# Triangle layer t1: the mask goes into the operand of the projection instead of the product behind it

## The reference, cut to what matters

```python
def _L1_conv_ref(z, mask, w_ap, b_ap, w_ag, b_ag, w_bp, b_bp, w_bg, b_bg, w_g, b_g, w_z, b_z, ...):
    m = mask[..., None]
    zn = _layer_norm(z, ln_in_w, ln_in_b)
    a = (zn @ w_ap + b_ap) * jax.nn.sigmoid(zn @ w_ag + b_ag) * m
    b = (zn @ w_bp + b_bp) * jax.nn.sigmoid(zn @ w_bg + b_bg) * m
    x = jnp.einsum('bikc,bjkc->bijc', a, b)
    x = _layer_norm(x, ln_out_w, ln_out_b) @ w_z + b_z
    g = jax.nn.sigmoid(zn @ w_g + b_g)
    return x * g
```

## Time and profile before

| | us |
|---|---|
| median of the runs (3) | 526.87 |
| lowest and highest of them | 526.49, 528.16 |
| the profiled execution, its own time | 530.72 |
| its span in the profile | 528.9 |
| its granted TensorE clock, mean | 0.89 |

### The profile page before, as it was taken

One profiled execution on the slowest core, in us unless ns is written; L12 is line 12 of the kernel. 1 busy time (PEld: TensorE's weight loads), 2 busy tenths in 40 slices (PEclk: granted clock), 3 DMA queues, 4 the chain that ended last, 5 costly groups with the idle time before them and its releaser, 6 DMA issues.

```text
span 528.9 us, 8984 instructions
## 1 busy us (share of the span) xinstructions
PE 426.9 (81%) x3226; PEld 326.1 (62%) x3226; DVE 360.4 (68%) x1170; ACT 235.4 (44%) x577; POOL 250.6 (47%) x315
## 2 busy tenths in 40 slices
PE   3698867987798877998499968698598857869995
PEld 2466754566345753896399945598455846836664
DVE  4977688647996488547534458301968498998885
ACT  1597554620775546677300038476379543300000
POOL 4899288003985186000000035000879168269994
PEclk9999998778798989999589979799579996569999
DMA  9400000000000000000000000000000000001223
GB/s 171 84 2 1 1 1 0 1 3 0 1 2 1 0 2 0 1 2 2 1 0 1 1 2 1 0 2 2 0 1 2 1 0 1 2 0 20 42 45 55
DMA packets 34671, 6.05 MB, mean 11 GB/s; under 512 B 33713, under 2 KB 34369, under 8 KB 34626
## 3 DMA queue, kind: packets, MB, share of 16 engines
q1 hardware_dynamic: 34626, 5.46, 5.9%
HBM read 3.36 MB, written 2.10 MB: 10 GB/s over the span
## 4 chain that ended last, share of the span: by engine, by line
PE 53%; DVE 32%; ACT 5%; POOL 4%; issue 3%; DMA 1%; SPq 1%; DVEq 0%; POOLq 0%
PE psum L1606 7%; DVE moments L339 6%; PE psum L605 5%; PE psum L1179 5%; PE psum L1178 5%; DVE ab L762 4%; PE psum L476 4%; PE psum L634 3%; PE psum L645 3%; PE psum L1779 3%; DVE ab L746 3%; POOL z L401 2%; PE psum L1799 2%; PE psum L1784 2%; PE psum L1201 1%
## 5 line engine op out<-in xcount | busy, mean ns | idle before, releaser
L325 POOL TENSOR_TENSOR z<-x_cols,moments 128x496 f32<-128x496 f32 x28 | 30.4, 1086 | 80.6 <-DVE moments L339 80.6
L605 PE MATMUL psum<-wp_L,z_t 64*128 64x320 f32 x384 | 65.3, 472 | 1.3 <-DVE ab L762 0.9
L476 PE MATMUL psum<-ident,z 128*128 128x128 f32 x224 | 45.0, 339 | 21.4 <-POOL z L401 15.2
L339 DVE BATCH_NORM_STATS2 moments<-x_cols 128x6 f32<-128x64 f32 x448 | 60.9, 207 | 2.0 <-ACT x_cols L885 1.8
L476 PEld LDWEIGHTS psum<-ident,z 128*128 128x128 f32 x224 | 32.2, 174 | 45.1 <-POOL z L401 27.4
L605 PEld LDWEIGHTS psum<-wp_L,z_t 64*128 64x128 f32 x384 | 34.9, 196 | 26.0 <-issue 23.1
L378 ACT ACTIVATE z_t<-psum 128x512 f32<-128x512 f32 x56 | 40.2, 719 | 21.3 <-PE psum L476 20.8
L1314 ACT ACTIVATE ab<-psum,mv 128x128 f32<-128x128 f32 x108 | 39.7, 368 | 16.2 <-PE psum L1179 5.9
L824 POOL TENSOR_TENSOR gate<-gate,stats 128x512 f32<-128x512 f32 x24 | 25.2, 1049 | 45.2 <-DVE stats L787 44.8
L1179 PE MATMUL psum<-ab,R_vt 128*128 128x128 f32 x216 | 45.7, 294 | 0.0
L645 PE MATMUL psum<-wo_L,z_t 64*128 64x128 f32 x384 | 30.4, 301 | 18.5 <-DVE x_cols L795 11.5
(11 more groups left out here) (271 smaller groups left out, 894.7 us busy)
## 6 DMA issues: line engine op xcount, KB each, us to landing
x_cols<-in_x_dram SPq DMA_DIRECT2D x16, 128.0 KB, 2.9
out_dram<-x_rows SPq DMA_DIRECT2D x32, 64.0 KB, 1.9
par<-in_par_dram SPq DMA_DIRECT2D x1, 644.5 KB
w<-in_w_dram SPq DMA_DIRECT2D x4, 64.0 KB, 2.3
w<-in_w_dram SPq DMA_DIRECT2D x1, 256.0 KB, 2.5
mask<-in_mask_dram SPq DMA_DIRECT2D x1, 64.0 KB, 3.1
row<-in_row_dram SPq DMA_DIRECT2D x1, 3.3 KB
w_bias<-in_w_dram SPq DMA_DIRECT2D x1, 8.0 KB, 1.8
```

The source lines that it names most:

```text
L339: m = dve.bn_stats(moments[:, q, k:k + 2, :].rearrange("p k m -> p (k m)"), X4[:, SQ * q + s, g:g + 2, :].rearrange("p g c -> p c g"))
L476: m = pe.transpose(bank(b % 2)[:, k * N:(k + 1) * N], block_of(Z)(4 * b + k), ident[:, :])
L605: m = pe.matmul(bank(slot_bank(s) + h, 2 * 5 * C), ZT[rows, s, :], wp[l][rows, :, :], start=True, stop=True)
```

## The change

The mask is applied before the projection. Since a masked linear part is (zn @ w + bias) * m, and the bias goes through the operand too (one of the channel columns of `z` is set to ones, L396, so that a masked operand masks the bias as well), the linear columns can be computed from a masked copy of ZT. For this the mask has to lie as ZT does, channels on partitions and positions along the row, the same on all 32 channels:

- TensorE transposes the mask once (in `tri_weights_pe` of t1), and VectorE copies the result to `mask_turned` (in `tri_weights2_dve` of t1).
- SyncE stores it to a DRAM buffer of 64 KB, and after f0 has read its pooled values, four transfers read it back, each spread over 32 partitions, 32 x 4096, into the tile `gate` (MASK_WIDE). Step s of the loop later overwrites just the columns whose masked block was made.
- `masked_turned(eng, b)` multiplies a block of ZT by MASK_WIDE into the tile `squares` (ZTM): blocks 0 to 2 on VectorE, each ahead of product s = b, blocks 3 to 7 on GpSimd, each ahead of a gate pair.
- `project(s)` of t1 waits for masked block s//4 and makes three calls instead of one for each row half: sigmoid columns (2x64) and gate columns (2x32) from ZT, linear columns (2x64) from ZTM.
- The product of t1 is the one operation of t0 and t3.

```diff
@@ -134,6 +134,8 @@
         par = sb("par", [GC, NPAR])
         row = sb("row", [1, NROW])
         mask = sb("mask", [N, N])
+        mask_turned = sb("mask_turned", [N, N])
+        mask_rows = nc.dram_tensor("mask_rows_dram", (N, N), F32, kind="Internal").ap()
         stats = sb("stats", [N, 4, N])
         moments = sb("moments", [N, Q, SQ * G, 3])
         ident = sb("ident", [N, N])
@@ -285,6 +287,9 @@
         for L, first, ahead_of in ((t0, 3, (1, 3, 5, 8, 11)), (t1, 3, (1, 3, 5, 8, 11)), (t3, 5, (2, 4, 7))):
             L.turned_first, L.turn_ahead = first, {s: first + k for k, s in enumerate(ahead_of)}
         f0.outputs_of, r1.outputs_of = t0, t1
+        mask_ps, mask_copied = t0.s["bt_ps"], t0.s["bt_dve"]
+        zm_dve, zm_pool = t0.s["bt_dve"], t0.s["bt_act"]
+        mask_rows_in, mask_wide_in = x_in[0], x_in[1]
         t3.banks_free = x_done(r2)
         f3.early_banks_free = [output_read(t3, S // 4 - 3)]
         f3.banks_free = [output_read(t3, S // 4 - 1)]
@@ -562,6 +567,9 @@
             dve.tensor_copy(wo[l][:, 1, :], cent[:, :]).then_inc(sm, 1)
             if L is t0:
                 dve.tensor_copy(gate_cent[:, :], bank(L.wbank)[:, 320:320 + E0]).then_inc(f0.s["w_gate"], 1)
+            if L is t1:
+                dve.wait_ge(mask_ps, C // 4 + 1)
+                dve.tensor_copy(mask_turned[:, :], bank(L.wbank)[:, 352:352 + N]).then_inc(mask_copied, 1)
 
         def tri_weights_pe(pe, L):
             l = L.name
@@ -573,6 +581,9 @@
             pe.matmul(bank(L.wbank)[:, 192:320], cent[:, :], wotmp[l][:, 0:GC], start=True, stop=True)
             if L is t0:
                 pe.matmul(bank(L.wbank)[:, 320:320 + E0], cent[:, :], pcol("gate"), start=True, stop=True)
+            if L is t1:
+                pe.wait_ge(par_in, PAR_LOADS)
+                pe.transpose(bank(L.wbank)[:, 352:352 + N], mask[:, :], ident[:, :]).then_inc(mask_ps, 1)
             fold_biases(pe, bank(L.wbank)[:, 0:5 * C], scaled[l][:, :], prow(f"{l}_b"), lnb_at[l][:, :], pcol(f"{l}_w", C))\
                 .then_inc(L.s["w_pe"], 1)
 
@@ -589,6 +600,22 @@
             o = slot_bank(s) * BANK
             return PSUM[:, o:o + 2 * BANK].rearrange("p (h f) -> p h f", h=2)[:, :, 0:2 * 5 * C]\
                 .rearrange("p h (g w) -> p h g w", g=2)
+
+        MASK_WIDE = GATE[:, :].rearrange("p (s n) -> p s n", s=S)
+        ZTM = SQR[:, :].rearrange("p (s n) -> p s n", s=S)
+        ZM_DVE = 3
+
+        def masked_turned(eng, b):
+
+            eng.wait_ge(mask_wide_in, 16 * G + 16 * G)
+            eng.wait_ge(t1.s["zt"], t1.at["zt"] + b + 1)
+            done = zm_dve if b < ZM_DVE else zm_pool
+            eng.tensor_tensor(ZTM[:, 4 * b:4 * b + 4, :], ZT[:, 4 * b:4 * b + 4, :], MASK_WIDE[:, 4 * b:4 * b + 4, :],
+                              ALU.mult).then_inc(done, 1)
+
+        def masked_at(b):
+
+            return (zm_dve, C // 8 + 2 + b) if b < ZM_DVE else (zm_pool, C // 8 + 1 + b - ZM_DVE)
 
         def tri_pe(pe, L):
             l = L.name
@@ -600,10 +627,16 @@
                     pe.wait_ge(L.s["lin"], L.at["lin"] + s - SLOTS + 2)
                 if s > last:
                     pe.wait_ge(L.s["lin"], L.at["lin"] + s - SLOTS + 1)
+                if L is t1:
+                    pe.wait_ge(*masked_at(s // 4))
                 for h in range(2):
                     rows = slice(h * HALF_ROWS, (h + 1) * HALF_ROWS)
-                    m = pe.matmul(bank(slot_bank(s) + h, 2 * 5 * C), ZT[rows, s, :], wp[l][rows, :, :],
-                                  start=True, stop=True)
+                    if L is t1:
+                        for w, z in ((slice(0, 2 * C), ZT), (slice(4 * C, 5 * C), ZT), (slice(2 * C, 4 * C), ZTM)):
+                            m = pe.matmul(slot(s)[:, h, :, w], z[rows, s, :], wp[l][rows, :, w], start=True, stop=True)
+                    else:
+                        m = pe.matmul(bank(slot_bank(s) + h, 2 * 5 * C), ZT[rows, s, :], wp[l][rows, :, :],
+                                      start=True, stop=True)
                 m.then_inc(L.s["proj"], 1)
 
 
@@ -739,28 +772,18 @@
             eng.tensor_tensor(x, x, x_of(L)[:, 4 * b:4 * b + 4], ALU.add)\
                 .then_inc(L.s["xb"], 1)
 
-        def masked_product(dve, s):
-
-            for g in range(G):
-                w = slice(g * 2 * C, (g + 1) * 2 * C)
-                m = dve.scalar_tensor_tensor(out=to_ab(s)[:, g, :], in0=slot(s)[:, g // 2, g % 2, 2 * C:4 * C],
-                                             scalar=mask[:, g * S + s:g * S + s + 1], in1=SIG[:, s % SLOTS, w],
-                                             op0=ALU.mult, op1=ALU.mult)
-            m.then_inc(t1.s["lin"], 1)
-
         def x_block(L, b):
 
             return by_block(L.src)[:, 4 * b:4 * b + 4]
 
         def tri_dve(dve, L, after):
             for s in range(S):
+                if L is t1 and s < ZM_DVE:
+                    masked_turned(dve, s)
                 dve.wait_ge(L.s["sig"], L.at["sig"] + s + 1)
                 sig = SIG[:, s % SLOTS, :].rearrange("p (h g w) -> p h g w", h=2, g=2)
-                if L is t1:
-                    masked_product(dve, s)
-                else:
-                    dve.tensor_tensor(to_ab(s).rearrange("p (h g) w -> p h g w", h=2), slot(s)[:, :, :, 2 * C:4 * C], sig,
-                                      ALU.mult).then_inc(L.s["lin"], 1)
+                dve.tensor_tensor(to_ab(s).rearrange("p (h g) w -> p h g w", h=2), slot(s)[:, :, :, 2 * C:4 * C], sig,
+                                  ALU.mult).then_inc(L.s["lin"], 1)
             if L is t0:
                 for b in range(1, C // 4, 2):
                     turn_copy(dve, L, b, BT[:, 4 * b:4 * b + 4, :], "bt_dve", "bt_ps")
@@ -813,6 +836,8 @@
         def tri_pool(pool, L, after):
             pool.wait_ge(L.s["w_dve"], L.at["w_dve"] + TRI_W)
             for b in range(S // 4):
+                if L is t1 and b + ZM_DVE < S // 4:
+                    masked_turned(pool, b + ZM_DVE)
                 gate_bias(pool, L, b)
                 add_x(pool, L, b)
             pool.wait_ge(L.s["xb"], L.at["xb"] + S // 4)
@@ -1974,6 +1999,13 @@
             sp.dma_start(w1_bias[:, :], w1_d[C:C + 1, :, :].rearrange("o e h -> (o e) h")).then_inc(par_in, 16)
             sp.dma_start(w2[:, :, :], w2_d).then_inc(par_in, 16)
             sp.dma_start(w2l[:, :], w2l_d).then_inc(par_in, 16)
+            sp.wait_ge(mask_copied, C // 8 + 1)
+            sp.dma_start(mask_rows, mask_turned[:, :]).then_inc(mask_rows_in, 16)
+            sp.wait_ge(mask_rows_in, 16 * G + 16)
+            sp.wait_ge(f0.s["pool_ps"], f0.at["pool_ps"] + 1)
+            for g in range(G):
+                sp.dma_start(MASK_WIDE[g * C:(g + 1) * C, :, :],
+                             mask_rows[g * S:(g + 1) * S, :].unsqueeze(0).to_broadcast([C, S, N])).then_inc(mask_wide_in, 16)
             out4 = out_d.rearrange("(g s) j c -> j g s c", g=G)
             for b in range(S // 4):
                 sp.wait_ge(f3.s["done"], f3.at["done"] + 2 * b + 2)
```

## The result

| | before | changed |
|---|---|---|
| median, us | 526.68 (4 runs) | 538.15 (4 runs) |
| lowest and highest | 525.19, 528.16 | 537.38, 538.78 |
| ratio, 95% interval | | 1.0204 [1.0161, 1.0247] |
| span of the profiled execution | 528.9 | 537.0 |

The change costs 11.5 us; the forecast was +2.0, with a range up to 537.0. The direction was right, the size was not.

What follows compares the result with a forecast made beforehand. VectorE was taken to bound the second half of the t1 stage, with TensorE replacing it. Copy near f0 +0.3, t1 stage +3.3, L634 -1.6: net +2.0, 528.9 us; range 525.6 to 537.0.

Steps and rivals of the forecast that it cites:

- half level at the start: TensorE at t1's start: after idling, the clock starts at half level, costing 2.5 us (1.95 to 3.05).
- 32p + turns + last pass: TensorE in t1's loop: 32 steps of p, five turns of 0.59 us, then a last pass of 0.26.
- masked block 0: VectorE ahead of t1's loop: the first 128x512 mask product takes 1.0 us, bounds 0.69 and 1.40.
- t1 later as a whole: Around gating layer f0, ahead of t1: VectorE's added mask copy delays later work by 0.3 us.
- p: TensorE's time per step in t1's loop: six weight loads of 0.113, 0.68 us, at most 0.82.
- L978: TensorE row of 4-column passes with 128-column weights, 0.113 us apart; taken as the price of one weight load.
- The first rival: t1's row halves do not run beside each other: 0.90 or 1.13 a step, 536.0 or 543.3 us; chance 0.13 + 0.12.
- The wait: At t1's start TensorE waits for VectorE's first masked block; first projection at 141.4, not 137.09.
- late and slow start: Start of t1's loop: first projection delayed by the masked block, then half clock; costs about 7 us together.
- L634: TensorE's outer product after t1's loop: near 7.4 us instead of 9.05, counted as -1.6.
- one copy near f0: VectorE copies the turned mask once behind t1's weight copies: 0.28 us, counted as +0.3.
- the transfers: Mask to DRAM and 2 MB spread back: there before 131, first read at 140.3, cost nothing.

Runs made afterwards that it cites:

- e5: The changed kernel plus five extra 512-column matmul calls filling TensorE's wait for the first masked block: 533.35 us, 1.0092 against the kernel before.
- e1: The kernel before with only t1's projection split into three calls per row half, no wait or mask transfer: 541.1 us, 1.0217.
- e2: The changed kernel with one 320-column call per row half again, all from the masked operand: 526.56 us, 0.9987 against the kernel before.
- e3: The changed kernel with two calls per row half, 192 columns from ZT and 128 from ZTM: 527.13 us, 1.0008 against the kernel before.
- e9: The changed kernel with each gate call widened from 64 to 128 columns, still twelve passes a step: 534.23 us, 1.0126 against the kernel before.
- e10: The changed kernel with a step's six calls alternating between the row halves: 530.79 us, 1.0060 against the kernel before.
- e8: The kernel before without t1's mask, one unmasked product a step: 519.41 us, 0.9867.
- e6: The changed kernel with two calls per row half and the first block as in the kernel before: 524.71 us, 0.9950 against the kernel before.
- e4: The changed kernel with steps 0 to 3 as in the kernel before, six calls from step 4: 524.87 us, 0.9948 against the kernel before.
- e7: The changed kernel with two calls per row half, two blocks as before, all six masked blocks on GpSimd ahead of its gate pairs: 522.85 us, 0.9889 against the kernel before.

## Why the prediction failed, step by step

The forecast put the end of the loop at 148.4 + 32 x 0.68 = 170.2; the trace has 182.18, 12.0 later. The pieces, in the forecast's own terms:

| term | forecast | measured | late by |
|---|---|---|---|
| half level at the start | 2.5 | 10.1 (change against e5) | 7.6 |
| loop at full level, 32p + turns + last pass | 25.0 | 28.1 (e5) | 3.1 |
| masked block 0 | 1.0 | 1.50 | 0.5 |
| t1 later as a whole (turn at 136.86, not 136.08) | 0.3, counted apart | 0.8 | 0.8 |

Most of the last row belongs to the execution and not to the change: VectorE is 0.6 later already at 108.64, ahead of the added copy (108.05 before).

**The step that failed is "half level costs half of such a stretch: 1.95 to 3.05, I take 2.5".** Its stretch, 4 to 6 us, was read from loops of 320-column passes and carried over to passes of 64 and 128 columns. Shown: the level (e5), that the three calls per half draw it out with or without the late start (e1), that longer passes end it early (e2, e3, e9), and that the order of the calls counts too (e10). What decides it on the chip is not shown. Nor is it known why it ended after 22 us. In all four loops of short passes that begin at half level the clock rose within 0.6 us ahead of a turn (164.7 in the change, 158.2 in e1, 148.4 in e9, 153.1 in e10), but earlier turns of the same loops passed without it; whether the two belong together was not tested.

**p was right, the sum over it was not.** 0.666 a step against 0.68; that the weight loads set it, as L978 had it, fits e9. But the sum let the passes run on over five turns, with one last pass of 0.26 at the end. The loop has seven groups (e9's rows show a break after step 13 too), each with 0.52 once: 32 x 0.666 + 5 x 0.59 + 7 x 0.52 = 27.9, near the 28.1. The first rival, the halves that do not run beside each other, was wrong for the steady run and right for the ends of groups: 0.32 of the 0.52 there goes when the halves take turns (e10). The Trainium skill, "TensorE: Matmul & The Clock Gate", says in its step-by-step section that matmuls stay in program order; by the prediction's estimate that would have been 1.13 a step. The trace does not agree with it for calls on different row halves: a step takes 0.666, and a pass of the lower half starts ahead of two of the upper (e5).

**The wait was right in place and near in size.** VectorE's L613 ends TensorE's idle time, at 142.56. It took 1.50, outside the bounds; the two masked blocks after it took 0.67, below the lower one. The late and slow start was put at about 7 together; without the short passes it is 5.6 (e2 against e8).

**Right as forecast:** L634 at 7.42; one copy near f0 (0.28 long, later work moved by 0.2); the transfers, landed by about 123 with nothing waiting for them. GpSimd ended at 185.4 and not near 175, since the loop it follows was slow, but nothing waited for it (its next work is at 196.21). GpSimd's last masked block (ready at 175.0) was not waited for in the slow loop, but it is in the faster loops of e6.

The rest of the network gave part of it back: behind the outer product, the same code took 353.0 us in the profiled execution of before (175.90 to the end) and 347.4 in the changed one; over all kernels here 346 to 353 (351.5 in e5, 350.8 in e9). So of the +13.7 at the end of the stage (189.63 against 175.90) the two profiled spans keep +8.1 (528.9 to 537.0). The medians differ by 11.5, since the profiled execution of before was 4.0 above its median and the changed one 0.6. In the same way e5 and e9 gain less in all than in the stage. Whether the length of that part is chance or follows from when the loop ends was not tested; single runs of the unchanged kernel lie up to 11 us apart.

## What to carry to other kernels

Splitting a matmul call to give some of its columns another operand multiplies the weight loads; price each load, and keep the columns of one operand side by side so that there are as few calls as operands (e3 costs nothing here, the change 2%). A half clock read from one loop isn't the half clock of another: ask what the new loop does from a start at half level, and let its first steps be the long passes (e4, e7). When the calls on each of two row halves are split, alternating the halves is worth a try (e10, with three calls each; not tried with two).

## What the runs showed of the hardware

- From a granted 0.50, passes of 320, or of 192 and 128 columns were at full level after 3.4 to 6.3 us; the split loop of 128, 64 and 128 columns after 21.7 and 22.7; with the halves alternating after 9.3, with 128 columns throughout after 6.6. At full level the same short passes stayed there for 23 and 28 us, to the loop's end (e4, e5).
- Two row halves run beside each other even with three calls of one half queued ahead of the other: 0.666 us for twelve passes, with 0.32 lost once in each group.
- The same 128x512 product took VectorE 1.50 us at 141.05, while GpSimd ran 128x496 products (140.72 to 143.45), and 0.67 at 145.97, when GpSimd was idle.
